# Unread fp32 products of 512 columns in each step of an exposed recurrence (one core, early-fusion model)

## What is computed

```
h = h + _L1_attn_ref(_layernorm(h), ...)          # attention, rows i attend to j < i
h = h + _L1_ffn_ref(_layernorm(h), ...)           # the recurrence

def step(carry, xs):                              # 96 steps, h and c are 64 x 64
    h, c = carry
    i_t = sigmoid(xi_t + h @ V_i)
    g_t = tanh(xg_t + h @ V_c)
    o_t = sigmoid(xo_t + h @ V_o)
    c_new = h * c + i_t * g_t
    h_new = o_t * tanh(c_new)
    return ((h_new, c_new), h_new)
```

## Time and profile before

| | us |
|---|---|
| median of 3 runs | 873.36 |
| lowest and highest of them | 864.75, 876.89 |
| the profiled execution | 867.51 |
| its span on the core | 865.8 |
| TensorE busy (products) | 702.4 (81%) |
| VectorE busy | 533.9 (62%) |
| ScalarE busy | 360.0 (42%) |
| GpSimd busy | 252.1 (29%) |

### The profile page before, as it was taken

One profiled execution on the slowest core, in us unless ns is written; L12 is line 12 of the kernel. 1 busy time (PEld: TensorE's weight loads), 2 busy tenths in 40 slices (PEclk: granted clock), 3 DMA queues, 4 the chain that ended last, 5 costly groups with the idle time before them and its releaser, 6 DMA issues.

```text
span 865.8 us, 16453 instructions
## 1 busy us (share of the span) xinstructions
PE 702.4 (81%) x6414; PEld 416.6 (48%) x6414; DVE 533.9 (62%) x1104; ACT 360.0 (42%) x667; POOL 252.1 (29%) x223
## 2 busy tenths in 40 slices
PE   4687887853689999787989999788899887776775
PEld 3674654543522222253334442366477665555554
DVE  4856577569684655374886766268667673556443
ACT  2232444423334555444445555425555434232332
POOL 4248575549100314020430304025223230011000
PEclk9999788965599999899999999769999978555555
DMA  9730000000063433001222322000000000000000
GB/s 191 139 70 5 2 1 1 1 1 0 7 191 113 139 113 114 2 2 37 89 71 86 97 88 66 5 2 2 2 2 2 2 1 5 7 11 7 11 8 13
DMA packets 42402, 36.85 MB, mean 43 GB/s; under 512 B 20888, under 2 KB 29848, under 8 KB 42328
## 3 DMA queue, kind: packets, MB, share of 16 engines
q1 hardware_dynamic: 41242, 35.57, 15.3%
q10 hardware_dynamic: 1088, 0.26, 0.2%
HBM read 33.85 MB, written 1.97 MB: 41 GB/s over the span
## 4 chain that ended last, share of the span: by engine, by line
PE 58%; DVE 22%; ACT 7%; issue 5%; POOL 3%; DMA 2%; SPq 1%; POOLq 0%; DVEq 0%; ACTq 0%
PE PS L1569 10%; PE PS L1556 10%; PE PS L1532 6%; PE PS L1603 4%; PE PS L1582 3%; PE PS L1651 3%; PE PS L1662 3%; PE PS L1518 2%; DVE XC L925 2%; PE PS L1624 2%; PE PS L1320 2%; PE PS L1635 2%; PE PS L1329 2%; DMA BIG<-in_x 2%; DVE st L907 1%
## 5 line engine op out<-in xcount | busy, mean ns | idle before, releaser
L1569 PE MATMUL PS<-Y,W1f 64*128 64x512 f32 x384 | 109.8, 650 | 4.4 <-DVE Y L1066 2.9
L1556 PE MATMUL PS<-XC,w2s 128*64 128x512 f32 x384 | 104.0, 622 | 0.6 <-ACT XC L709 0.6
L1532 PE MATMUL PS<-LS,V 64*64 64x32 f32 x1140 | 70.9, 270 | 38.5 <-DVE LS L1195 38.5
L709 ACT ACTIVATE XC<-PS 128x1024 f32<-128x1024 f32 x68 | 69.4, 1021 | 59.4 <-PE PS L1556 48.6
L1532 PEld LDWEIGHTS PS<-LS,V 64*64 64x64 f32 x1140 | 58.9, 188 | 71.0 <-DVE LS L1195 64.3
L1066 DVE TENSOR_TENSOR Y<-XD,UF 128x512 f32<-128x512 f32 x96 | 70.2, 743 | 17.0 <-DMA UF<-gd 9.1
L566 POOL TENSOR_TENSOR Y<-XC 128x512 f32<-128x512 f32 x12 | 14.0, 1166 | 173.1 <-DVE XC L1046 173.1
L1182 DVE SCALAR_TENSOR_TENSOR LS<-LS 128x32 f32<-128x32 f32 x96 | 21.8, 227 | 56.6 <-ACT LS L807 43.4
L1556 PEld LDWEIGHTS PS<-XC,w2s 128*64 128x64 f32 x384 | 19.2, 135 | 73.8 <-issue 61.2
L1569 PEld LDWEIGHTS PS<-Y,W1f 64*128 64x128 f32 x384 | 29.5, 187 | 51.5 <-issue 27.9
L178 POOL TENSOR_TENSOR st<-st,mhalf 128x8 f32<-128x8 f32 x24 | 39.3, 1637 | 37.8 <-DVE st L910 37.8
(11 more groups left out here) (236 smaller groups left out, 1474.7 us busy)
## 6 DMA issues: line engine op xcount, KB each, us to landing
UF<-gd SPq DMA_DIRECT2D x192, 128.0 KB, 2.9
BIG<-in_x SPq DMA_DIRECT2D x8, 512.0 KB, 12.0
out<-X SPq DMA_DIRECT2D x48, 32.0 KB, 2.0
W1f<-in_L_ffn_w SPq DMA_DIRECT2D x2, 512.0 KB, 6.3
EX<-in_L_ffn_w SPq DMA_DIRECT2D x1, 1024.0 KB, 15.2
H<-in_txt SPq DMA_DIRECT2D x2, 256.0 KB, 12.2
w2s<-in_L_ffn_w SPq DMA_DIRECT2D x1, 512.0 KB, 9.5
gd<-EX SPq DMA_DIRECT2D x6, 64.0 KB, 1.7
```

Of the source, the lines that this page charges most:

```text
L709: act.activation(Hb[:, b:b + 2, :], PS[:, b:b + 2, :], ACT.Relu).then_inc(S("m_h"), 1)
L1532: mm = pe.matmul(PS[r, b, o:o + HN], V3[r, g, :], HB[r, (t - 1) % 4, :], start=False, stop=True, skip_group_check=True)
L1556: mm = pe.matmul(PS[64 * h:64 * h + 64, 6, :], w2s[:, 2 * p + h, :], Hb[:, n % 2 * 2 + h, :], start=(p == 0), stop=(p == E // 2 - 1))
L1569: mm = pe.matmul(PS[:, n % 2 * 2 + h, :], W1f[r, 2 * p + h, :], Rb[r, n % 4, :], start=True, stop=True)
```

## The change

In each slot of the exposed recurrence but the last, after the step's own products and ahead of the residual's, TensorE computes one product of W1f[:, 0, :] (128x128) with 512 columns of w2s, in fp32, into PSUM bank 1; where t % 4 = 1 it computes two. Nothing reads the result, no semaphore is raised by it, and it waits for none. The operands are real weights that lie in SBUF. These are 63 + 16 = 79 products.

```
                 if t is None and step_at(g + 1) is not None:
                     gates_x(step_at(g + 1) // 4, (0, 1, 2))
+                if g >= LS1 and t < T - 1:
+
+                    for n in range(2 if t % 4 == 1 else 1):
+                        pe.matmul(PS[:, 1, :], W1f[:, 0, :], w2s[:, 0:8, :].rearrange("p e d -> p (e d)"), start=True, stop=True)
                 if 10 <= g < 16:
```

## The result

| | before | changed |
|---|---|---|
| median (us) | 875.12 (4 runs, 864.75 to 880.53) | 884.44 (4 runs, 882.01 to 893.69) |
| profiled execution, span (us) | 867.51, 865.8 | 882.01, 880.3 |
| first to last recurrent product of the exposed steps (us) | 130.9 | 147.2 |
| four plain steps (us) | 7.67 | 8.27 |

The ratio is 1.0156, with a 95% interval of 1.0102 to 1.0210: the changed kernel is slower by 1 to 2%. In the profiled executions the span grew by 14.5 us and the exposed recurrence by 16.3, so all of it lies there; the part ahead of it was 1.3 us shorter and the tail 0.5. (The first record of L1532 starts at 728.51 before and at 727.22 after.

A forecast was written before the change was run, and what follows sets the result against it. The exposed recurrence's step chain (1.90 us, TensorE at 1.2 GHz) was taken as the bound, TensorE's own work afterwards. 4.4 - 1 + 1.5 + 3 - 0.4 = plus 7.5 us on a mean of 870.6 gave 878 us, range 865 to 897.

The forecast's parts named there:

- The clock rises: Exposed recurrence: the 512-column products were expected to bring the granted clock to 1.00 some 5 us after it begins.
- Rival 3: Exposed recurrence: the new products do not raise the clock, which stays where it was; about 978 us, chance 0.03.
- A step becomes TensorE's own work: Exposed steps at the high clock: TensorE's work, 1.80 to 2.34 us, exceeds the 1.69 us chain and sets the step.
- The plain steps: The 49 step distances without residual work beside them: 98.3 us against 93.9, four steps 8.00 against 7.67; plus 4.4 us.
- Rival 1: New products in the exposed steps are cheaper, 0.86 us each, and hide; 867 us, chance 0.20.
- The start: First steps of the exposed recurrence: the clock falls and the second step takes 4.2 us; plus 1.5 us, bounds 0 and 4.
- The disturbed steps: 14 distances in two places beside the residual's normalisation, set by DVE and POOL: shorter work there gives minus 1 us together.
- (b): Two places beside the residual: TensorE idles, the clock may fall for two steps, 2.5 us; plus 3 us, bounds 0 and 6.
- The tail: End of the kernel: the last recurrent product and last turning of the output run at the high clock; minus 0.4 us.
- Rival 2: Exposed recurrence: the clock toggles, a quarter of the time at 1.2 GHz; 892 us, chance 0.17.
- The bound: Exposed recurrence: the high clock shortens the chain by 0.21 us over 63 distances, at most 13.2 us, 1.5% of the time.

## Why the prediction was right

The direction, the place and the mechanism were as forecast, and the time, 884.4 us, lies in the range and 6 us above the forecast of 878. That it came so close is in part luck: in the profiled executions the change costs plus 14.5 us where the sum has plus 7.5, and the exposed recurrence alone plus 16.3 where its terms have plus 7.9. By its steps, in those executions:

- **The clock rises.** Right: 1.00 in 740 to 760 us where it was 0.50. Rival 3 is gone. The experiments with 256 and with 32 columns show what would have made it true: TensorE busy all the time at 0.50.
- **A step becomes TensorE's own work.** Right, and shown three ways: the chain rows above, the 1.69 us when the second product is left out, and the 0.86 us for each one added to a step that has one. ScalarE's tanh starts 0.47 us after the recurrent product, as in the forecast.
- **The plain steps**, forecast plus 4.4 us: measured plus 7.3 (a set 8.27 us, not 8.00). This term was mis-sized. The new product costs 1.05 us from start to start when the 64x32 product follows, the upper bound, not the middle of 1.01: four times 0.04. Nearly all of the rest is in the input products, 0.59 and 0.36 us where 0.54 and 0.32 were read beside the recurrent product. A 128x128 product follows them here, not the recurrent one, which is the likely reason; no run separates it. (At t = 94 there are no input products, and the sum counts them: 1.68 us and not 2.02.) Rival 1 (0.86 for each) is refuted by the same rows.
- **The start**, forecast plus 1.5: measured plus 1.6. All five kernels with two products ahead went without this fall, but so did two executions without them, so it was a term of chance, as the sum had it.
- **The disturbed steps**, forecast minus 1 for the shorter work and plus 3 for falls, so plus 2: measured plus 7.4, 3.7 in each place. This is the main miss, the term (b). I let the clock fall with a chance of six tenths, and for two steps, 2.5 us. It fell at both, and stayed low through three steps, of which t = 48 has the turning of the chunk and t = 49 two new products: 11.1 us for the three, 4.3 more than with the waits filled. The cure points to the cause: with the wait filled both falls vanish and each place is some 4.1 us shorter. It is one execution of each kernel, and the kernel with two products in every step passed the first chunk unfilled without a fall, so the wait makes a fall likely rather than certain. (The prediction took the two places of before as equal, at 18.75 us; the first takes 18.4. And its 131.5 us, from the earlier trace rows, end 0.6 us behind the start of the last step.)
- **The tail**, forecast minus 0.4: from the last recurrent product to the end of the span 5.9 us instead of 6.4, minus 0.5. The part ahead of the recurrence was 1.3 us shorter in this execution, which the change cannot do.
- **Rival 2**, toggling for a quarter of the time: the granted clock is at 0.50 in three stretches that are together 24 of 147 us, 16% of the recurrence. It was the right mechanism at a smaller size. With 384 columns it would have been the result, and gone further: 0.50 for most of the recurrence in the execution profiled. With 256 throughout it is rival 3's case.

The bound was worth the most: 13.2 us was all that the clock could give back, and the added work ate more than that. With the work cut so that the steps need little more than the chain (7.30 us a set against four times 1.69), there is a gain of some 1%, of which 5.8 us are seen in the recurrence.

## What to carry to other kernels

Work that is added only to keep TensorE's clock up is worth at most what TensorE's part of the dependent chain shrinks by at the high clock, here 0.21 us a step, and stands in the same queue as the work it is to speed up: size it to the idle time that remains at the high clock, step by step, and not to that of the low clock. Put it first where TensorE waits longest, since one fall costs more than the saving of many steps; and look at the granted clock in the profile after every cut, because a little less work can turn the kernel from slightly faster to 3% slower by the median (448 and 384 columns). Profile more than one execution, since the falls differ between executions of the same instructions.

## What the runs showed that I had not expected

- The same instructions can run at either level of the clock: with 384 columns a set took 7.18 us at 1.00 or 11.7 us at 0.50, and four runs spread from 871.5 to 915.6 us. At 0.50 TensorE was busy for 75 us without a pause and the clock still did not rise.
- The fp32 product of 128x128 by 32 columns costs 0.46 us at 1.2 GHz, as eight records at 0.23 each show, nearly all of it weight loads. By columns it would be a sixteenth of one of 512, which costs 1.85 there (two in a row 3.71, in the kernel with two in every step); it is a quarter.
- The code ahead of the recurrence is the same in nearly all of these kernels, and its length differed by 14 us between executions (the first exposed product starts at 727.2 in the changed kernel and at 741.4 in the one with short products). That is as much as the effect under study. The length goes with the clock: the granted clock ahead of the recurrence was 0.90 in the kernel before and the changed one, the two shortest, and 0.88 in the longest. A plain set inside a profile read 8.27 us in three different kernels that share it, so stretches of one profile were the better measure for a plain step. For a whole recurrence they are less so, since a fall of the clock more or less is some 4 us.
